# A gated mixture-of-experts stage on one core: all eight shared blocks beside the routing, the final sum alone at the end

## The reference, cut to what matters

```python
def _L1_ffn_ref(x, gate_w, W1, W2, Ws1, Ws2):   # D=256, H=192, E=8, K=2, NS=2
    def _gated_mlp(x, w1, w2):
        h = x @ w1.T
        y, g = jnp.split(h, 2, axis=-1)
        return y * jax.nn.silu(g) @ w2.T
    xf = x.reshape(-1, D)                        # 4096 tokens
    scores = jax.nn.softmax((xf @ gate_w.T).astype(jnp.float32), axis=-1)
    top_vals, top_idx = jax.lax.top_k(scores, K)
    w_dense = zeros.at[arange(T)[:, None], top_idx].set(top_vals)
    h = jnp.einsum('td,ehd->teh', xf, W1)
    y, g = jnp.split(h, 2, axis=-1)
    eo = jnp.einsum('teh,edh->ted', y * jax.nn.silu(g), W2)
    z = jnp.einsum('te,ted->td', w_dense, eo)
    return (z + _gated_mlp(xf, Ws1, Ws2)).reshape(x_shape)
...
x = x + jnp.tanh(g_ffn[1]) * _L1_ffn_ref(_layernorm(x, axis=-1), ...)
```

## Time and profile before

| | us |
|---|---|
| median of 3 runs | 1096.27 |
| lowest, highest | 1092.83, 1097.70 |
| profiled execution | 1098.07 |
| its span | 1096.3 |
| PE busy in the span | 962.1 (88%) |
| DVE busy | 776.9 (71%) |
| ACT busy | 575.6 (53%) |
| POOL busy | 355.6 (32%) |

### The profile page before, as it was taken

One profiled execution on the slowest core, in us unless ns is written; L12 is line 12 of the kernel. 1 busy time (PEld: TensorE's weight loads), 2 busy tenths in 40 slices (PEclk: granted clock), 3 DMA queues, 4 the chain that ended last, 5 costly groups with the idle time before them and its releaser, 6 DMA issues. The chain is left out here.

```text
span 1096.3 us, 22536 instructions
## 1 busy us (share of the span) xinstructions
PE 962.1 (88%) x6381; PEld 811.3 (74%) x6381; DVE 776.9 (71%) x2237; ACT 575.6 (53%) x1349; POOL 355.6 (32%) x551
## 2 busy tenths in 40 slices
PE   4999999999996679999999999854888889999973
PEld 3667666676764358999999999844777779999862
DVE  3677777777752436888888888855766658888767
ACT  1588888878884423443444434316355266556520
POOL 1011111111110013453444534422776514444410
PEclk9999999999998859999999999986989899999996
DMA  6776758576700400010010100201433214444267
GB/s 164 153 147 146 152 119 161 118 159 139 167 1 23 132 26 25 26 50 25 25 50 25 44 31 25 74 1 48 128 124 102 92 54 125 130 126 127 85 221 239
DMA packets 85873, 104.40 MB, mean 95 GB/s; under 512 B 15070, under 2 KB 75438, under 8 KB 85808
## 3 DMA queue, kind: packets, MB, share of 16 engines
q1 hardware_dynamic: 77616, 81.91, 30.4%
q0 software_dynamic: 7632, 21.05, 5.4%
q10 hardware_dynamic: 560, 0.66, 0.2%
HBM read 38.50 MB, written 57.62 MB: 88 GB/s over the span
## 5 line engine op out<-in xcount | busy, mean ns | idle before, releaser
L1604 POOL DMA_INDIRECT expert_out<-early_weights,aim x71 | 69.9, 985 | 101.6 <-DVE aim L1933 57.7
L1142 ACT ACTIVATE f_hidden<-c_hidden,f_b 128x256 f32<-128x256 f32 x128 | 53.7, 471 | 68.2 <-PE c_hidden L1331 68.2
L1595 POOL DMA_INDIRECT sorted_rows<-m_z,slot_i x64 | 71.8, 1122 | 44.4 <-DVE slot_i L1813 26.6
L1329 PE MATMUL c_mlp<-f_w_hi,f_hidden_hi 128*128 128x256 f32 x256 | 80.7, 315 | 3.6 <-DVE f_hidden_lo L1260 3.6
L1329 PE MATMUL c_hidden<-y2T_hi,f_w_hi 128*128 128x256 f32 x256 | 77.1, 301 | 0.0
L1331 PE MATMUL c_mlp<-f_w_hi,f_hidden_lo 128*128 128x256 f32 x256 | 72.4, 283 | 0.0
L1330 PE MATMUL c_mlp<-f_w_lo,f_hidden_hi 128*128 128x256 f32 x256 | 72.4, 283 | 0.0
L1331 PE MATMUL c_hidden<-y2T_hi,f_w_lo 128*128 128x256 f32 x256 | 72.2, 282 | 0.0
L1330 PE MATMUL c_hidden<-y2T_lo,f_w_hi 128*128 128x256 f32 x256 | 72.2, 282 | 0.0
L748 PE MATMUL ps_probT<-ident,prob 128*77 128x128 f32 x512 | 68.8, 279 | 3.8 <-ACT prob L479 3.3
L596 DVE TENSOR_REDUCE mx<-ps_scores 128x8 f32<-128x616 f32 x64 | 50.9, 796 | 28.0 <-PE ps_scores L682 27.9
(11 more groups left out here) (334 smaller groups left out, 3093.5 us busy)
## 6 DMA issues: line engine op xcount, KB each, us to landing
sorted_rows<-no_row SPq DMA_DIRECT2D x15, 2322.0 KB, 13.4
m_z<-sorted_rows SPq DMA_DIRECT2D x71, 129.0 KB
early_weights<-expert_chunks SPq DMA_DIRECT2D x8, 640.0 KB, 4.2
combT<-combineT_all SPq DMA_DIRECT2D x16, 256.0 KB, 2.3
slT<-slots_all SPq DMA_DIRECT2D x16, 256.0 KB, 2.5
early_weights<-expert_out SPq DMA_DIRECT2D x8, 512.0 KB, 6.3
early_weights<-expert_out POOLq DMA_DIRECT2D x8, 512.0 KB, 6.2
out<-x_all SPq DMA_DIRECT2D x8, 512.0 KB, 3.4
```

Source lines behind the costliest of these rows:

```text
L1142: last = act.activation(hf[:, q % 2, j, :], psH[:, q % 2, j, :], ACT.Relu, bias=fb1[:, c_:c_ + 1])
L1329: pe.matmul(out, lh, rh, start=start, stop=False, skip_group_check=shared)
L1595: pool.indirect_dma_start(out=sorted_rows[:, :], in_=zn[:, s % 3, t, :], in_offset=None, out_offset=bass.IndirectOffsetOnAxis(ap=slot_i[:, ...
L1604: pool.indirect_dma_start(out=expert_out[:, :], in_=xo[:, i % 3, :], in_offset=None, out_offset=bass.IndirectOffsetOnAxis(ap=aim_i[:, i % ...
```

## The change

All eight blocks' shared units move beside the routing (`FIRST` is every block), so that a step has three units instead of two, and one unit is left behind step 7. The code for LAST goes: the two normalizations on ACT, the turnings behind the expert tiles and the unit loops of the tail on every engine. The rows read back get a buffer for each block, in the memory of the expert weights (`x_weights_hi`, `x_weights_lo`), which nobody needs any more by then. So SP and POOL post eight reads each at once, without waiting for sums, and SP posts its eight writes behind them. `combine` waits for its block's `result` and its two reads.

```diff
-        back = early[:, 0:2 * 2 * BT * D].rearrange("p (s i n) -> p s i n", s=2, i=2)
+        spare = [w[:].rearrange("p e n -> p (e n)").bitcast(F32) for w in (eh, el)]
+        back = [spare[c // 4][:, c % 4 * 2 * BT * D:(c % 4 + 1) * 2 * BT * D].rearrange("p (i n) -> p i n", i=2) for c in range(NBLK)]
...
-        FIRST, LAST = [0, 1, 3, 4, 6, 7], [2, 5]
-        TURN = FIRST + LAST
+        FIRST = list(range(NBLK))
+        TURN = FIRST
...
-            return [u for u in range(2 * s - 1, 2 * s + 1) if u >= 0] if s < NBLK else list(range(2 * NBLK - 1, BESIDE))
+            return [u for u in range(SC * s - 1, SC * s + 2) if 0 <= u < BESIDE]
...
             for c_, b in enumerate(TURN):
-                if c_ >= 2:
-                    sp.wait_ge(sum_done.sem, 2 * (c_ - 2) + 1)
-                sp.dma_start(back[:, c_ % 2, 0], kept[:, 0, b]).then_inc(back_in[0][c_ % 2].sem, 16)
-                if c_ >= 1:
-                    sp.wait_ge(sum_done.sem, 2 * c_)
-                    sp.dma_start(Y[:, TURN[c_ - 1]], X[:, TURN[c_ - 1]]).then_inc(o_out.sem, 16)
-            sp.wait_ge(sum_done.sem, 2 * NBLK)
-            sp.dma_start(Y[:, TURN[-1]], X[:, TURN[-1]]).then_inc(o_out.sem, 16)
+                sp.dma_start(back[c_][:, 0], kept[:, 0, b]).then_inc(back_in[0][c_].sem, 16)
+            for c_, b in enumerate(TURN):
+                sp.wait_ge(sum_done.sem, 2 * (c_ + 1))
+                sp.dma_start(Y[:, b], X[:, b]).then_inc(o_out.sem, 16)
...
             for c_, b in enumerate(TURN):
-                if c_ >= 2:
-                    pool.wait_ge(sum_done.sem, 2 * (c_ - 2) + 2)
-                pool.dma_start(back[:, c_ % 2, 1], kept[:, 1, b]).then_inc(back_in[1][c_ % 2].sem, 16)
+                pool.dma_start(back[c_][:, 1], kept[:, 1, b]).then_inc(back_in[1][c_].sem, 16)
...
-            act.wait_ge(sent[2].sem, 16 * 2 * BT * 2)
-            apply(LAST[0], 2).then_inc(zn_done.sem, 1)
...
-                if i == BT:
-                    act.wait_ge(sent[1].sem, 16 * 2 * BT * 3)
-                    apply(LAST[1], 1).then_inc(zn_done.sem, 1)
...
-                if m % SC == 0 and m not in (0, BESIDE):
+                if m % SC == 0 and m:
                     result(m // SC - 1)
...
             def combine(c_):
                 b = TURN[c_]
+                dve.wait_ge(res_done.sem, c_ + 1)
...
-            z_lo_turned(0)
-            for m in range(BESIDE, NBLK * SC):
-                hidden(m)
-                hidden_lo(m)
-                if m == BESIDE:
-                    z_lo_turned(1)
-                combine(m - BESIDE)
-            result(NBLK - 1)
-            combine(NBLK - 2)
-            combine(NBLK - 1)
+            for c_ in range(NBLK):
+                combine(c_)
...
-            turn_last(0)
-            for m in range(BESIDE, NBLK * SC):
-                up(m)
-                if m == BESIDE:
-                    turn_last(1)
-                else:
-                    down(m - 1)
-            down(NBLK * SC - 1)
```

More of the change, by code:

```diff
@@ L1509, in phase_d @@
         xo_out = [sig(f"x_sent{j}", 1, 16) for j in range(3)]
-        back_in = [[sig(f"m_back_in{i}{j}", 1, 16) for j in range(2)] for i in range(2)]
+        back_in = [[sig(f"m_back_in{i}{j}", 1, 16) for j in range(NBLK)] for i in range(2)]
         sum_done, o_out = sig("m_sum", 2), sig("m_o_out", 1, 16)
-        FIRST, LAST = [0, 1, 3, 4, 6, 7], [2, 5]
-        TURN = FIRST + LAST
+        FIRST = list(range(NBLK))
+        TURN = FIRST
         BESIDE = len(FIRST) * SC
         def units(s):
-            return [u for u in range(2 * s - 1, 2 * s + 1) if u >= 0] if s < NBLK else list(range(2 * NBLK - 1, BESIDE))
+            return [u for u in range(SC * s - 1, SC * s + 2) if 0 <= u < BESIDE]
         kept = expert_out.rearrange("(i j p t) d -> p i j (t d)", i=2, j=NBLK, p=P)
@@ L1736, in _ @@
                     x_out(i - 2)
[L1738 to L1744, removed]
-            for m in range(BESIDE, NBLK * SC):
-                silu(m)
-                hidden_hi(m)
-                if m == BESIDE:
-                    z_turned(1, 0)
-                    z_turned(1, 1)
         @block.vector
@@ L1977, in _ @@
             dve.wait_ge(gate_w.sem, 3)
[L1979 to L1984, removed]
             def combine(c_):
                 b = TURN[c_]
+                dve.wait_ge(res_done.sem, c_ + 1)
                 for i in range(2):
-                    dve.wait_ge(back_in[i][c_ % 2].sem, 16 * (c_ // 2 + 1))
+                    dve.wait_ge(back_in[i][c_].sem, 16)
                     if i == 1:
@@ L1993, in combine @@
                         n = b * BT + t
-                        last = dve.scalar_tensor_tensor(out=X[:, b, t, :], in0=back[:, c_ % 2, i, t * D:(t + 1) * D], scalar=gw[:, n, i:i + 1],
+                        last = dve.scalar_tensor_tensor(out=X[:, b, t, :], in0=back[c_][:, i, t * D:(t + 1) * D], scalar=gw[:, n, i:i + 1],
                                                         in1=X[:, b, t, :], op0=ALU.mult, op1=ALU.add)
                     last.then_inc(sum_done.sem, 1)
-            z_lo_turned(0)
-            for m in range(BESIDE, NBLK * SC):
-                hidden(m)
-                hidden_lo(m)
-                if m == BESIDE:
-                    z_lo_turned(1)
-                combine(m - BESIDE)
-            result(NBLK - 1)
-            combine(NBLK - 2)
-            combine(NBLK - 1)
+            for c_ in range(NBLK):
+                combine(c_)
         @block.tensor
@@ L2091, in _ @@
                     down(m - 1)
-                if not others:
-                    logits(s + 1)
             down(BESIDE - 1)
@@ L2167, in _ @@
             pe.wait_ge(xo_ev.sem, XT)
-            def turn_last(q):
-                pe.wait_ge(zn_done.sem, NBLK + q + 1)
-                if q:
-                    pe.wait_ge(zl_done.sem, len(FIRST) + q)
-                for k in range(KD):
-                    for t in range(BT):
-                        out = psT[:, t * P:(t + 1) * P] if k == 0 else psR[:, t, :]
-                        last = pe.transpose(out, zn[:, 2 - q, t, k * P:(k + 1) * P], ident[:])
-                    last.then_inc(zt_mm.sem, 1)
-            turn_last(0)
-            for m in range(BESIDE, NBLK * SC):
-                up(m)
-                if m == BESIDE:
-                    turn_last(1)
-                else:
-                    down(m - 1)
-            down(NBLK * SC - 1)
 def spread(ap, dim, n):
```

## The result

The changed kernel takes 1115.06 us, median of 4 runs (1110.74 to 1116.74), against 1095.88 for the kernel before on the same chip: a ratio of 1.0172, 95% interval 1.0133 to 1.0211. The forecast was 1113 with a range of 1105 to 1124.

The account below looks back on a forecast made before the run. The prediction took a routing step to be TensorE work, then a 4.30 us chain on other engines. From 1098.07, +25.9 +2.0 +4.6 -0.5 -15.3 gave 1114.8, less 1.8 for this execution: 1113, range 1105 to 1124.

Parts of the forecast that it names:

- The step: Routing: a steady step grows from 12.48 to 18.47 us, with a 2.81 hole; all steps together add 25.9.
- The clock: Routing: half-clock starts add 2.0 us behind step 0's hole and 4.6 behind three of five step-end holes.
- Step 2's hole: Routing: statistics and a shared result delay the products, so the next turning comes at 801.05, +2.07 us.
- The hole that the table causes: End of the routing: the tile table on VectorE holds a unit up as before, with a hole of 4.32 us.
- Expert tiles: Two applies leave ScalarE, the second within the expert tiles: -0.5 us, between 0 and -2.1.
- The tail: After the last scatter: shared work and pairwise posting go, 16 reads posted at once; -15.3 us, between -7.6 and -17.0.
- Holes filled: Rival: new units fill TensorE's free time, routing grows by 2.3 us, kernel takes 1083; chance 0.05.
- holes partly filled: Rival: each unit costs 4.29 less 0.95 us, routing grows by 20.0, kernel takes 1100.5; chance 0.08.
- Full clock in the long steps: Rival: the routing's holes of 2.8 us cost no clock, kernel takes 1108.5; chance 0.2.
- Half clock after every hole, and a mixed tail: Rival: slow starts add 3.1 us and mixed reads and writes 7.7, kernel takes 1124; chance 0.17.
- the reads go at once: Tail: all 16 reads are posted at once; its rival, a queue taking only a few, would cost 1 or 2 us.

Follow-up runs that it names:

- e1_logits_late: The changed kernel with logits behind the last up of a step instead of behind the first other up on TensorE; 1098.33 us, ratio 1.0026 to the kernel before.
- e2_rows_early: The changed kernel with rows_in ahead of the step's last silu and rounding on ScalarE; 1091.93 us, ratio 0.9979 to the kernel before.
- e3: The changed kernel with nine unused matmuls filling the hole at the end of each step that a turning follows; 1104.94 us, ratio 1.0107 to the kernel before.
- again_after: The changed kernel timed once more, on another chip; 1112.23 us, ratio 1.0161 to the kernel before.
- e8: The kernel before with rows_in ahead of the step's last silu and rounding on ScalarE; 1091.34 us, ratio 0.9971 to the kernel before.
- e9: The kernel before with rows_in earlier on ScalarE and the statistics later on VectorE; 1092.96 us, ratio 0.9984 to the kernel before.
- e11: The kernel before with rows_in earlier, all reads at once, the tile table and the expert weights' remainders later; 1089.05 us, ratio 0.9936.
- e6: The changed kernel with rows_in earlier on ScalarE and the statistics of blocks 4 to 7 behind the other units on VectorE; 1092.21 us, ratio 0.9975.
- e4_pairs: The changed kernel with the former pairwise reads into two buffers per queue, shared work still out of the tail; 1124.76 us, ratio 1.0277.
- e5_reads_alone: The kernel before with eight buffers and all reads issued at once, two blocks' shared work left in the tail; 1092.38 us, ratio 0.9982.

## Why the prediction was right, point by point

**The step.** Its core was 18.47 for a steady step and a hole of 2.81; the trace has 18.45 and 18.44, and 2.74. Lengthenings by step, measured: +7.82, +5.76, +1.98, +3.94, +5.96, +6.38 and, from 868.24 to the expert tiles, +0.38 (48.37 against 47.99). The forecast without the clock: +7.57, +3.04, +2.07, +3.96, +5.99, +4.84 and 2.76 - 4.29 = -1.53. e1_logits_late and e2_rows_early show the mechanism, not just the size. In the last of these stretches two things cancel: the hole behind the table is 1.39 longer, and the half clock behind it shorter (granted 0.50 from 868.40 to 875.10 in before, from 903.40 to 906.70 in after).

**The clock.** Three stretches at 1.2 GHz account for the differences in steps 1 and 5 and for most of that in step 6. From the opening turning of a step to the next are 3.30 at the full clock (792.20 to 795.50); they were 6.03 behind the hole of 4.75 (+2.7, forecast +2.0), and 4.86 and 4.85 behind two of the holes of 2.74 (+1.56 and +1.55). The forecast had three such of five; there were two. Together 5.8 against 6.6. The first was taken too small and the other group too large, so the two errors cancel in part, and that is luck.

**Small errors in place.** Step 2's hole came in two pieces, one of them (808.11) a down that waits for a block's result; the length was right, 19.14 against 19.23. The hole that the table causes is 5.71, not 4.32, since it now also holds a result up.

**Expert tiles.** -0.5 was too small a gain, and in after (156.54) the clock hid it. In its profile the first 4 us of that stretch and the next were granted 0.55 and 0.60 of the clock, in before 0.65 and 0.92. Profiles with like clocks show what the code that left this part costs, the two applies above all: with 0.66 to 0.69 and 0.89 to 0.91, e1 to e3 take 154.99 to 155.02, 1.6 below before; with 0.54 or 0.55 and 0.59 to 0.61, after and again_after take 156.54 and 156.06, and e8, e9 and e11, which still have it, 157.83 to 158.49. So the term is -1.3 to -2.4, and the slower start took about as much back.

**The tail.** Right in form: one write train behind the reads, sums back to back. Of the terms, POOL's first read landed 6.9 after its issue, not 5.5, and VectorE waited 2.32 more after the first sums. A block took 3.36 (from 1080.47 to 1105.66 for 7.5 blocks) and not 3.44. The end is 35.85 after the first read, where the forecast had 36.8. The bound was VectorE's: its last sum ended at 1105.66, 3.3 before the end.

**The sum.** The changed parts of the profiles grew by 32.22 - 0.10 - 16.22 = 15.9, where the forecast had 16.7. The medians differ by 19.2, and the 3.3 beyond that show in no profile, so that 1113 came within 2 us of 1115.06 is in part luck.

**The rivals.** "Holes filled" and "holes partly filled" asked for a routing longer by 2.3 and 20.0; it is 32.22. "Full clock in the long steps", 1108.5, is excluded by the 4.86 and 4.85 above. "Half clock after every hole, and a mixed tail" fell with two full-clock starts of four behind 2.74 and with 385 GB/s. That the reads go at once shows in the issues of SP, eight within 4 us.

**What the forecast didn't see**: that 18.1 of the 32 us were the price of one place in ScalarE's queue. It had the idle VectorE and ScalarE in its rows, and took the position of rows_in as given.

## What to carry to other kernels

When work moves into a stage whose steps end in a chain between engines, ask on which side of the chain's start it lands: ahead of it, it costs its full length and uncovers the chain as well. Then look for the chain's producer in its in-order queue. If it stands behind work that waits for the latest result, move it ahead (here 18 us for one move with three units in a step, 5 with two), and expect the next chain to come up after it, as e6 and e8 show; measure after every move. Buffers for all reads pay in full only when nothing else stands between the sums, and freeing the sums pays in full only when the rows lie ready.

## What was not expected of the hardware

- Sixteen reads and eight writes in two queues ran at 402 GB/s and then 385, where the windows of before have 406, 349 for a write alone and 296 for the two mixed.
- Of four holes of 2.73 to 2.74 us before otherwise equal steps, two were followed by a stretch at 1.2 GHz and two were not, and in again_after and e4_pairs, whose routing is the same code, it fell on the same two, the third and the fourth. In e8_before_rows one followed a hole of 1.96 (793.56 to 798.43, 4.87 instead of 3.30). The turning at 839.60 in before, behind 2.10, had one (4.82 to the next); the same turning in e5_reads_alone, behind 2.11, had none (838.33 to 841.63, 3.30). In e3_fill the one behind 2.71 had none either (771.41 to 774.71). So the length of the hole alone doesn't decide it. No hole of 0.96 or less in e1_logits_late was followed by one. What does was not found.
- Of the sixteen reads, SP's landed 3.2, 10.4 and 17.7 us after their issue (least, median, most), POOL's 6.9, 13.9 and 19.3, though both queues had eight of the same size.
